# Layer 0 of a two-layer decoder from the output projection to the experts as one pipeline over token tiles, with dense experts on one-hot masked rows

## Chip, cores and metric

The kernel runs on one NeuronCore of a Trainium2 chip. The metric is the device time of one execution in microseconds (us). Engines are written as in the profile: PE (matrix multiply; PEld is its weight load), DVE (vector), ACT (activation), POOL (GpSimd), SP (the queue that issues most DMAs).

## What is computed

The input x is 2 x 1024 tokens of 256 features in fp32. Two decoder layers follow each other; each is self-attention, cross-attention on 77 context tokens, and a mixture of 8 experts. Layer 0, cut to what the change touches:

```python
x = x + L0_attn(_layernorm(x))          # ... @ Wo + bo at its end
# cross-attention: 16 heads of 16, 77 keys, only the 32 largest scores of each row count
scores = einsum('bhsd,bhnd->bhsn', Q, K) / SCALE
topk_scores, idx = top_k(scores, 32)
x = x + (softmax(topk_scores) @ V[idx]) @ Wo.T + bo
# experts: the router picks one of 8 for each token
h = _layernorm(x)
probs = softmax(h @ router_w.T + router_b)
y = (h @ expert_w[argmax(probs)].T + expert_b[argmax(probs)]) * max(probs)
x = x + y
```

Layer 1 (causal attention, cross-attention with a layer norm, experts with a hidden layer of 1024) is not changed, apart from the first step of its first layer norm.

## The kernel before, in words

The 2048 tokens are T = 16 tiles of 128. All tensors of the chip's memory are pieces of one big tile `arena`; all matmul results go to `banks`, 8 banks of 128 x 512 fp32. Every engine has its own list of instructions, in the order in which the code emits them, and waits by named counters (`sem(...)`); there is no scheduler. Layer 0 after the attention consists of five stages, and in most of them every tile is finished before the next stage begins:

1. `project(block, 0)`: per tile PE turns the attended rows (L1087), ACT copies them (L1108), PE multiplies with Wo (L1098), DVE adds the result to x (L1115) and takes the row statistics (L402).
2. `ln(block, "ln1", ...)`: for all 16 tiles mean and variance (L418), root on ACT (L438), normalized rows h (L425), turned on PE (L470) and copied to hT (L441); `add_bias` adds the output bias to x on POOL (L486).
3. `cross(block, 0, top=True)`: a pipeline over tiles. PE makes queries (L1183) and scores (L1193), ACT copies the scores to `sc` (L1291). DVE finds the 32 largest of each head in `largest`: four rounds of `max` (L1359: the 8 largest of 77) and `match_replace` (L1364: strike them out), 16 heads each. Its result is `left`, the scores without the 32. POOL subtracts the maximum from both (L1316), ACT takes exp of both (L1298, L1279), and POOL subtracts one from the other (L1326), which leaves the weights of the 32. PE turns these in four groups of four heads (L1203), ACT copies each group (L1271), PE multiplies with V (L1212), turns the result (L1221), DVE divides by the sum (`normalize`, L1388 and L1395), and PE, ACT do the output projection (L1231 to L1239, L1308, L1310). DVE, ACT and POOL run tiles 4 to 13 in a hardware loop (`Fori`) of two tiles a round; PE's list is written out.
4. `ln(block, "ln2", ..., router=0)`: as ln1, with statistics of its own pass (L415), and router logits (L450, L457).
5. `moe(block, 0, ...)`: router choice and the position of every token in an order sorted by expert (DVE, L1612 to L1676), a scatter of the rows to DRAM (`sorted`, POOL L1684), then 23 tiles of sorted rows: load, turn (L1774), multiply with the expert's weights (L1812), bias (L1813), store to `expert_out`; and a gather back (POOL L1697), with gate and addition to x on DVE (L1867) and row statistics for ln3 (L402).

Then all engines meet at a barrier, and layer 1 begins with `ln(block, "ln3", ...)`.

Of the kernel before, what the change touches and what calls it, by code (L numbers as in the profile page):

```python
# [17 lines left out]
ALU = mybir.AluOpType  # L18
# [3 lines left out]
P = 128  # L22
# [5 lines left out]
C = 77  # L28
# [64 lines left out]
def build(nc, a, out):  # L93
    ctx = ExitStack()
    with ctx:
# [19 lines left out]
        xs_dram = [scratch(f"sorted{l}", [NS * P, D]) for l in range(2)]  # L115
        ys_dram = [scratch(f"expert_out{l}", [NS * P, D]) for l in range(2)]
# [18 lines left out]
        hmask = R.f32(8)  # L135
        wr = [R.f32(KD * E).rearrange("p (k e) -> p k e", k=KD) for _ in range(2)]
# [35 lines left out]
        CONST = 16  # L172
        W1_IN = 16 * 2
        ZW = 1024
        XS_CLEAR = 16 * 2 * -(-NS * D // ZW)


        def prepare(block):
# [6 lines left out]
            def _(sp):  # L185
# [28 lines left out]
                for l in range(2):  # L214
                    rows = xs_dram[l].rearrange("(p r) d -> p (r d)", p=P)
                    for n0 in range(0, NS * D, ZW):
                        w = min(ZW, NS * D - n0)
                        sp.dma_start(rows[:, n0:n0 + w], zero_tile[:, 0:w]).then_inc(sem("xs_clear"), 16)
# [3 lines left out]
            def _(pool):  # L222
# [3 lines left out]
                pool.memset(hmask, 1.0).then_inc(sem("const"), 1)  # L226
                for l in range(2):
                    pool.memset(xv[l][:, :, :, 0:HD], 0.0).then_inc(sem("const"), 1)
                    pool.memset(xv[l][:, :, :, HD:SLOT], 1.0).then_inc(sem("const"), 1)
# [4 lines left out]
                pool.wait_ge(sem("const"), 9)  # L234
# [11 lines left out]
                pool.wait_ge(sem("const"), 14)  # L246
# [873 lines left out]

        def cross(block, l, top):
# [369 lines left out]
        def moe(block, l, free_sem, free_val):  # L1491
# [187 lines left out]
            def _(pool):  # L1679
# [3 lines left out]
                for t in range(T):  # L1683
                    pool.indirect_dma_start(  # L1684
                        out=xs_dram[l], out_offset=bass.IndirectOffsetOnAxis(ap=posi[:, t:t + 1], axis=0),
# [8 lines left out]
                for t in range(T):  # L1694
                    if t >= NY:
                        pool.wait_ge(sem(s + "_x"), t - NY + 1)
                    pool.indirect_dma_start(  # L1697
                        out=yg[t % NY], out_offset=None, in_=ys_dram[l],
# [31 lines left out]
            def _(sp):  # L1730
                sp.wait_ge(sem(s + "_sc"), 16 * T)

                def load(t, r):
                    if late(t - NTB + 1):
                        sp.wait_ge(sem(s + "_tp"), t - NTB + 1)
                    sp.dma_start(xs[r], tile_rows(xs_dram[l], t)).then_inc(sem(f"{s}_xs{r}"), 16)

                def store(t, r):
                    if big:
                        sp.wait_ge(sem(s + "_yb"), t + 1)  # L1740
                        sp.dma_start(tile_rows(ys_dram[l], t), yb[r]).then_inc(sem(f"{s}_yst{r}"), 16)
# [85 lines left out]
            def _(act):  # L1827
                def step(t, r):
# [16 lines left out]
                    if not big and inside(t):  # L1845

                        act.wait_ge(sem(s + "_yb"), t + 1)
                        act.dma_start(tile_rows(ys_dram[l], t), yb[r]).then_inc(sem(f"{s}_yst{r}"), 16)
# [26 lines left out]
        with nc.Block() as block:  # L1875
# [54 lines left out]
```

## Time and profile before

| | us |
|---|---|
| median of 3 runs (lowest, highest) | 2024.06 (2022.25, 2025.41) |
| the profiled execution | 2022.71 |
| its span in the trace | 2020.9 |
| DVE busy over the span | 1287.8 (64%) |
| PE busy over the span | 1428.5 (71%) |
| ACT busy, POOL busy | 844.4, 412.3 |
| mean granted clock of PE | 0.855 of full speed |

The span runs from the first to the last instruction of the profiled execution; 1.8 us lie around it. Matmuls are pipelined, so the busy time of PE is not its work alone. The granted clock of PE has two levels, 1.00 (2.4 GHz) and 0.50 (1.2 GHz); a value between them is a mean over time.

### The profile page before, as it was taken

To read this page: it belongs to the slowest core of one execution; us is meant where nothing else is said; L and a number is where in the kernel's file an instruction comes from. 1 tells how busy PE (TensorE), PEld (TensorE's weight loads), DVE (VectorE), ACT (ScalarE), POOL (GpSimd) and SP (SyncE) were. 2 spreads that over 40 slices of the span, in tenths; PEclk is the share of its full clock that TensorE was granted. 3 is DMA by queue.
4 is the path that set the end of the run, shared out by engine and by line. 5 is a ranking of instruction groups with operands and counts; after the bars stand their busy time and mean duration, and the time that the engine had idled before them with its cause. 6 is when DMAs were issued, how large, how long until landed. Compare 5 with 4: busy or idle time off the path is not lost. (4 is left out here: it accounts for less than half of the span.)

```text
span 2020.9 us, 26349 instructions
## 1 busy us (share of the span) xinstructions
PE 1428.5 (71%) x8174; PEld 732.7 (36%) x8175; DVE 1287.8 (64%) x4686; ACT 844.4 (42%) x1674; POOL 412.3 (20%) x338
## 2 busy tenths in 40 slices
PE   4758999999884444444355395899987883379993
PEld 2421222222243333333233252333336672146662
DVE  6988878877328999999942446677744557501112
ACT  2731777777753232222221160566674562112110
POOL 2760000000003222222203333111111333200003
PEclk9965999999996776777776695899998996689997
DMA  7175133330000000000013349245400021650103
GB/s 252 58 200 76 23 47 45 46 45 9 24 1 1 1 1 1 1 1 1 1 43 112 91 140 172 38 68 69 59 2 0 12 40 35 240 169 27 31 23 91
DMA packets 122600, 116.09 MB, mean 57 GB/s; under 512 B 47010, under 2 KB 95966, under 8 KB 122468
## 3 DMA queue, kind: packets, MB, share of 16 engines
q1 hardware_dynamic: 116087, 103.12, 23.2%
q0 software_dynamic: 3072, 8.39, 1.4%
q10 hardware_dynamic: 3312, 3.02, 0.4%
q8 instruction: 62, 1.02, 0.2%
q14 instruction: 67, 0.55, 0.1%
HBM read 72.74 MB, written 41.49 MB: 57 GB/s over the span
## 5 line engine op out<-in xcount | busy, mean ns | idle before, releaser
L1051 DVE TENSOR_REDUCE arena<-banks 128x2 f32<-128x1024 f32 (+1 forms) x448 | 481.3, 1108 | 148.4 <-PE banks L898 93.3
L987 ACT ACTIVATE arena<-banks 128x512 f32<-128x512 f32 (+3 forms) x896 | 439.2, 556 | 186.5 <-PE banks L937 180.0
L898 PE MATMUL banks<-arena 96*128 96x512 bf16 (+3 forms) x896 | 285.7, 396 | 50.2 <-DMA arena<-v 22.2
L937 PE MATMUL banks<-arena 98*128 98x512 bf16 (+3 forms) x896 | 270.8, 362 | 9.9 <-ACT arena L987 7.5
L1203 PE MATMUL banks<-arena 128*77 128x128 f32 x512 | 85.8, 323 | 213.2 <-POOL arena L1326 207.0
L949 PE MATMUL banks<-arena 128*32 128x512 f32 (+3 forms) x1792 | 219.9, 563 | 12.8 <-ACT arena L987 6.7
L1364 DVE MATCH_REPLACE8 arena<-arena 128x77 f32<-128x77 f32 x1024 | 213.7, 223 | 0.0
L1316 POOL TENSOR_TENSOR arena<-arena 128x1232 f32<-128x1232 f32 x48 | 108.7, 2264 | 370.0 <-DVE arena L1364 258.3
L898 PEld LDWEIGHTS banks<-arena 96*128 96x128 bf16 x896 | 80.2, 102 | 233.8 <-DVE arena L1051 135.5
L1858 DVE COPY arena<-banks 128x1024 f32<-128x1024 f32 x23 | 28.2, 1225 | 205.0 <-PE banks L1797 205.0
L1359 DVE MAX8 arena<-arena 128x8 f32<-128x77 f32 x1024 | 149.5, 224 | 9.4 <-issue 7.3
L1203 PEld LDWEIGHTS banks<-arena 128*77 128x77 f32 x512 | 74.1, 180 | 224.5 <-POOL arena L1326 210.5
L937 PEld LDWEIGHTS banks<-arena 98*128 98x128 bf16 x896 | 81.9, 98 | 188.2 <-ACT arena L987 124.3
L486 POOL TENSOR_TENSOR arena<-arena 128x4096 f32<-128x4096 f32 x3 | 26.9, 8980 | 492.9 <-DVE arena L425 473.7
L1812 PE MATMUL banks<-arena 128*128 x460 | 111.8, 390 | 2.2 <-DVE arena L1858 1.4
L1271 ACT COPY arena<-banks 77x512 f32<-77x512 f32 x128 | 70.2, 584 | 100.1 <-PE banks L1203 100.1
L470 PE MATMUL banks<-arena 128*128 128x128 f32 x192 | 39.2, 372 | 100.6 <-DVE arena L425 99.7
L1193 PE MATMUL banks<-arena 128*128 128x308 f32 (+2 forms) x256 | 93.5, 519 | 4.6 <-ACT arena L1264 2.4
L1812 PEld LDWEIGHTS banks<-arena 128*128 128x128 f32 x460 | 84.7, 192 | 23.0 <-issue 12.7
L1015 POOL TENSOR_SCALAR_AFFINE_SELECT arena<-arena 128x512 f32<-128x512 f32 x64 | 40.6, 635 | 248.2 <-ACT arena L987 248.2
L1697 POOL DMA_INDIRECT arena<-expert_out,arena x32 | 31.4, 983 | 275.3 <-DMA expert_out<-arena 266.2
L1785 PE MATMUL banks<-arena 128*128 x184 | 84.7, 604 | 0.3 <-issue 0.3
(213 smaller groups left out, 2007.8 us busy)
## 6 DMA issues: line engine op xcount, KB each, us to landing
arena<-parts SPq DMA_DIRECT2D x192, 128.0 KB, 7.2
arena<-in_L_ffn_W SPq DMA_DIRECT2D x16, 1024.0 KB, 12.0
parts<-arena SPq DMA_DIRECT2D x24, 512.0 KB, 8.4
v<-arena SPq DMA_DIRECT2D x32, 256.0 KB, 2.3
arena<-v SPq DMA_DIRECT2D x16, 512.0 KB, 10.9
arena<-sorted SPq DMA_DIRECT2D x46, 128.0 KB, 2.1
sorted<-arena SPq DMA_DIRECT2D x10, 512.0 KB, 8.2
expert_out<-arena ACTq DMA_DIRECT2D x23, 128.0 KB, 2.3
```

The lines of the kernel that those rows point to most:

```text
L898: mm = pe.matmul(bank[:, 0:w], qst[r][0:KS, j, i * P:(i + 1) * P], kst[r][0:KS, j, kb * BANK:kb * BANK + w], start=True, stop=not diag)
L937: pe.matmul(bank, kst[r][0:KM, j, kt * P:(kt + 1) * P], qst[r][0:KM, j, half * BANK + lo:(half + 1) * BANK], start=True, stop=True).then_i ...
L949: mm = pe.matmul(PS[SLOT * j:SLOT * (j + 1), 7, lo:BANK], vst[u % NST][:, kt, j, :], prob[:, gi % 2 * G + j, lo:BANK], start=(kt == 0), st ...
L987: act.activation(prob[:, gi % 2 * G + j, lo:BANK], PS[:, 4 + n % 3, 0:BANK - lo], ACT.Exp, scale=SCALE).then_inc(sem(s + "_exp"), 1)
L1051: dve.tensor_reduce(m2[u % 2][:, 2 * pair:2 * pair + 2, i, kb], PS[:, 2 * (n % 2):2 * (n % 2) + 2, 0:w], AX.X, ALU.max).then_inc(sem(s + " ...
L1193: mm = pe.matmul(PS[:, bank, col:col + hn * C], qt[r][:, h0 // 8, :], kb.rearrange("p j c -> p (j c)"), start=True, stop=True)
L1203: mm = pe.transpose(PS[0:C, WB + c % 2, j * P:(j + 1) * P], ex[r][:, c * 4 + j, :], ident)
L1316: return pool.tensor_tensor(dst, src, m8[r][:, 0, :, 0:1].to_broadcast([P, NH, C]), ALU.subtract)
L1359: dve.max(m8[r][:, k, hd, :], src).then_inc(sem(s + "_m" if k == 0 else f"{s}_m{k}"), 1)
L1364: dve.match_replace(out=left[r][:, hd, :], in_to_replace=m8[r][:, k, hd, :], in_values=src, imm_value=LOWEST).then_inc(sem(f"{s}_k{k}" if ...
L1785: pe.matmul(PS[:, 2 + half, :], xsT[r][:, k, :], W1[:, bass.ds(e * (KD * F) + k * F + half * BANK, BANK)], start=(k == 0), stop=False)
L1812: pe.matmul(ps, lhs[:, k, :], W[:, bass.ds(e * (nk * D) + k * D, D)], start=(k == 0), stop=False)
```

## The change

`project`, `ln1`, `add_bias`, `cross`, `ln2` and `moe` of layer 0 are taken out and a new function `cross_experts` stands in their place, one pipeline over steps t = -3 to 19. In step t, the output projection works on tile t+3, the first layer norm on t+2, queries and scores on t+1, `largest` on t, the softmax and the weights on t-1, the output projection of the cross-attention on t-2, the second layer norm on t-3, and router and experts on t-4. All lists are written out, without a hardware loop.

The experts are computed without sorting: POOL multiplies the normalized rows of a tile with the one-hot choice, which gives 8 blocks of 256 columns that are zero where the token has another expert (`hm`, 128 x 2048), PE turns the 16 pieces (`turn_spread`), ACT copies them to `hmT`, and PE multiplies all 16 with the 8 experts' weights into one sum (`experts`); the bias comes from a matmul of the turned one-hot rows. The weights (2 MB) are loaded when the attention has ended, turned on PE and kept in place of `hT`. The rows of x for ln1 and ln2 are normalized on POOL, the root is taken on ACT for one tile at a time.

One buffer `sorted` and one `expert_out` are left (layer 1 uses them), so only one is cleared at the start. `ln3` takes its row statistics in a pass of its own, after the barrier.

```diff
-            project(block, 0)
-            ln(block, "ln1", "p0_x", T, stats_due=False)
-            add_bias(block, "ln1", xb_out, "w_in", W_IN)
-            cross(block, 0, top=True)
-            ln(block, "ln2", "x0_xd", T, router=0)
-            moe(block, 0, "x0_xd", T)
+            cross_experts(block)
 ...
-            ln(block, "ln3", "e0_x", T, stats_due=False)
+            ln(block, "ln3", "e0_x", T)
+        def cross_experts(block):
+                sp.wait_ge(sem(at + "_red"), NU * (len(fills(False)) + 3))
+                for e in range(E):
+                    sp.dma_start(raw[:, e], a["L0_ffn_expert_w"][e]...).then_inc(sem(s + "_we"), 16)
+            # PE
+                def turn_expert(e):
+                    if e == 0:
+                        pe.wait_ge(sem(s + "_we"), 16 * (E + 1))
+                def turn_h2(t):
+                    pe.wait_ge(sem(s + "_h2"), t + 1)
+                    pe.wait_ge(sem(s + "_hT1"), min(t + 6, T))
+                def logits(t):
+                    pe.wait_ge(sem(s + "_h2T"), t + 1)
+                def experts(t, part):
+                    if part == 0:
+                        pe.wait_ge(sem(s + "_n"), min(t + 3, T))
+                        pe.matmul(PS[:, OB, 0:D], ohT, bias, start=True, stop=False)
+                    pe.wait_ge(sem(s + "_hmT"), t * 4 + 2 * part + 2)
+                    for n in range(E * part, E * part + E):
+                        mm = pe.matmul(PS[:, OB, 0:D], hmT[:, n, :], WeT[:, n // KD, n % KD, :], ...)
+            # ACT, the end of its step
+                        copy_weights(t - 1, 2)
+                        copy_weights(t - 1, 3)
+                        exp_all(t)
+                        turned_h1(t + 2)
+                        turned_h2(t - 3)
+                        context(t - 1)
+            # POOL, its step
+                        less_max(left[(t - 1) % 2], left[(t - 1) % 2], t - 1).then_inc(sem(s + "_d2"), 1)
+                        pool.wait_ge(sem(s + "_oh"), t - 3)
+                        pool.tensor_tensor(hm, h2[n].unsqueeze(1).to_broadcast([P, E, D]),
+                                           oh[n].unsqueeze(2).to_broadcast([P, E, D]), ALU.mult)
+                        pool.tensor_tensor(ex[n], ex[n], left[n], ALU.subtract).then_inc(sem(s + "_w"), 1)
+                        normal(h1[t % 2], t, 0).then_inc(sem(s + "_h1"), 1)
+                        pool.tensor_tensor(x[:, t + 2, :], x[:, t + 2, :], xb_out, ALU.add)
+                        normal(h2[(t - 3) % 2], t, 1).then_inc(sem(s + "_h2"), 1)
+                        less_max(ex[t % 2], sc[t % 2], t).then_inc(sem(s + "_d"), 1)
+                        pool.tensor_tensor(x[:, t - 4, :], x[:, t - 4, :], yt[(t - 4) % 2], ALU.add)
+            # DVE
+                def router(t):
+                    dve.wait_ge(sem(s + "_lp"), t + 1)
+                    dve.tensor_tensor(lg[n], PS[:, QB, D:D + E], br[0], ALU.add)
+                def choose(t):
+                    dve.tensor_scalar(ta[n], lg[n], m1[n], None, ALU.subtract)
+                for t in range(FIRST, LAST):
+                        router(t - 4)
+                        row_statistics(t)
+                        choose(t - 4)
+                        aggregate(t)
+                        chosen(t - 4)
+                        largest(t, 0)
+                        sums(t - 2)
+                        inverse(t)
+                        normalize(t - 2)
+                        gates(t - 4)
+                        for k in range(1, 4):
+                            largest(t, k)
```

The list of PE in one step of the cross-attention before: a tile's queries (L1183), half of the weights' turns (L1203), scores (L1193), the other half, V (L1212), the turn of the result (L1221) and the output projection (L1231 to L1239).

```order
L1183 MATMUL banks<-arena 128x128 x4
L1203 MATMUL banks<-arena 77x128 x8
L1193 MATMUL banks<-arena 128x462
L1193 MATMUL banks<-arena 128x154
L1193 MATMUL banks<-arena 128x308 x2
L1203 MATMUL banks<-arena 77x128 x8
L1212 MATMUL banks<-arena 32x128 x16
L1221 MATMUL banks<-arena 128x128 x4
L1231 MATMUL banks<-arena 128x128 x2
L1235 MATMUL banks<-arena 128x256 x2
L1239 MATMUL banks<-arena 128x256
```

The same place in the changed kernel, the second half of a step t = 5 to 13: the turns of the masked rows (L1332), the turn of the mixed rows of tile t-2 (L1292) with its output projection (L1299, L1301), bias and expert matmuls of tile t-4 (L1340, L1343), the weights of tile t-1 (L1262), the turns of both layer norms (L1224, L1308), V (L1272) and the logits of tile t-3 (L1314).

```order
L1332 MATMUL banks<-arena 128x128 x8
L1292 MATMUL banks<-arena 128x128 x2
L1332 MATMUL banks<-arena 128x128 x8
L1299 MATMUL banks<-arena 128x256 x2
L1301 MATMUL banks<-arena 128x256
L1340 MATMUL banks<-arena 128x256
L1343 MATMUL banks<-arena 128x256 x8
L1262 MATMUL banks<-arena 77x128 x8
L1343 MATMUL banks<-arena 128x256 x8
L1262 MATMUL banks<-arena 77x128 x8
L1308 MATMUL banks<-arena 128x128 x2
L1314 MATMUL banks<-arena 128x8 x2
```

Thirty-three matmuls and turns of the experts now stand between the scores and the logits, and the logits, on which DVE's next step begins, are the last thing PE does in a step (the rows L1224 and L1272 beside the last two are left out).

DVE before, from the end of one tile to the first round of the next: the two rows of `normalize`, then `largest`.

```order
L1388 RECIPROCAL arena<-banks 128x16
L1395 TENSOR_TENSOR arena<-banks,arena 128x256
L1349 MEMSET arena 128x1
L1352 MEMSET arena 128x1
L1359 MAX arena<-arena 128x8 x16
```

DVE in the changed kernel, from the start of a step to its first round: the router (L1596, L1598, L1603 to L1607, L1612) and the statistics of two tiles (L1625, L1630).

```order
L1596 TENSOR_TENSOR arena<-banks,arena 128x8
L1598 TENSOR_REDUCE arena<-arena 128x1
L1625 BN_STATS arena<-arena 128x6 x2
L1603 TENSOR_SCALAR arena<-arena 128x8
L1604 SCALAR_TENSOR_TENSOR arena<-arena 128x8
L1607 TENSOR_REDUCE arena<-arena 128x1
L1630 BN_AGGR arena<-arena 128x2 x2
L1612 TENSOR_SCALAR arena<-arena 128x8
L1641 MEMSET arena 128x1
L1644 MEMSET arena 128x1
L1650 MAX arena<-arena 128x8 x16
```

Ten short instructions stand ahead of the first round now, and `normalize` has moved behind that round.

## Rows read from the trace of the kernel before

**Rows 1.** Stretches: us, busy us per engine, PEclk, DMA share, GB/s

```profile
618.70:1010.70 392.00, 157.28 (x1112) 118.56 (x1112) 374.96 (x3241) 114.77 (x193) 112.95 (x47) 0.72 0.00 1
1010.70:1157.20 146.50, 71.92 (x339) 44.57 (x339) 49.09 (x161) 28.17 (x63) 36.03 (x35) 0.72 0.28 85
```

The five busy times stand in the order PE, PEld, DVE, ACT, POOL, each with its count of instructions.

**Rows 2.** Waits of DVE from 618 to 1011: us, times, longest

```profile
DVE arena L1349 <- issue: 10.7, 4, 2.8
```

**Rows 3.** Timeline of DVE: start us, us, what (first round; two tiles' starts)

```profile
618.70 0.23 DVE L1359 MAX8 arena<-arena 128x8 f32<-128x77 f32 x1 [7.29 <-issue]
...
939.73 0.06 DVE L1349 MEMSET arena<- 128x1 f32 x1
...
963.67 0.06 DVE L1349 MEMSET arena<- 128x1 f32 x1
```

**Rows 4.** Groups by line over the whole span: busy us, mean ns, idle before

```profile
L1316 POOL TENSOR_TENSOR arena<-arena 128x1232 f32<-128x1232 f32 x48 | 108.7, 2264 | 370.0 <-DVE arena L1364 258.3 <-DVE arena L1376 110.9 <-DVE arena L1359 0.8
L1326 POOL TENSOR_TENSOR arena<-arena 128x1232 f32<-128x1232 f32 x16 | 44.5, 2784 | 21.4 <-ACT arena L1279 21.4
L1298 ACT ACTIVATE arena<-arena 128x1232 f32<-128x1232 f32 x32 | 39.7, 1240 | 6.4 <-POOL arena L1316 6.4
L1271 ACT COPY arena<-banks 77x512 f32<-77x512 f32 x128 | 70.2, 584 | 100.1 <-PE banks L1203 100.1
```

**Rows 5.** Timeline, DVE and POOL in layer 0's first projection

```profile
56.21 0.19 DVE L675 TENSOR_SCALAR arena<-arena 128x48 f32<-128x48 f32 x1
...
63.45 1.16 POOL L511 TENSOR_TENSOR arena<-arena 128x512 f32<-128x512 f32 x1
...
63.64 1.01 DVE L675 TENSOR_SCALAR arena<-arena 128x48 f32<-128x48 f32 x1
```

**Rows 6.** Stretches of 5 us, columns as in Rows 1 (PEclk third from right)

```profile
85.00:90.00 5.00, 3.45 (x12) 1.86 (x12) 4.93 (x7) 3.77 (x9) 3.78 (x5) 1.00 0.16 52
605.00:610.00 5.00, 3.29 (x19) 2.71 (x20) 4.65 (x20) 2.77 (x9) 0.00 (x0) 0.83 0.00 0
785.00:790.00 5.00, 0.00 (x0) 0.00 (x0) 4.87 (x39) 0.61 (x1) 2.26 (x1) 0.50 0.01 2
```

**Rows 7.** Timeline: matmuls and turns of PE, a table load of ACT

```profile
583.61 0.63 PE L912 MATMUL banks<-arena 128*128 128x128 f32 x4 [0.80 <-ACT arena L978]
...
601.29 1.89 PE L1098 MATMUL banks<-arena 128*128 128x256 f32 x8
...
606.71 5.81 PE L470 MATMUL banks<-arena 128*128 128x128 f32 x32 [3.52 <-DVE arena L425]
...
615.03 2.34 PE L1193 MATMUL banks<-arena 128*128 128x462 f32 x8 [0.71 <-ACT arena L1264]
...
622.88 1.28 ACT L1298 ACT_TABLE_LOAD   x1
...
624.18 1.23 ACT L1298 ACTIVATE arena<-arena 128x1232 f32<-128x1232 f32 x1
...
1590.81 1.04 PE L1203 MATMUL banks<-arena 128*77 128x128 f32 x8
```

**Rows 8.** Timeline: statistics, weights' DMA issues, short DVE work, around the barrier

```profile
1031.99 5.32 DVE L415 BATCH_NORM_STATS2 arena<-arena 128x6 f32<-128x256 f32 x16 [5.13 <-ACT arena L1310]
1032.35 4.02 SPq L1548 DMA_DIRECT2D arena<-in_L_ffn_expert_w  x8
...
1063.88 0.17 DVE L1662 TENSOR_TENSOR arena<-arena 128x8 f32<-128x8 f32 x1
1064.08 0.17 DVE L1663 TENSOR_SCALAR arena<-arena 128x8 f32<-128x8 f32 x1
...
1153.76 0.74 DVE L402 BATCH_NORM_STATS2 arena<-arena 128x6 f32<-128x256 f32 x2
...
1157.24 1.17 DVE L418 BATCH_NORM_AGGREGATE arena<-arena 128x2 f32<-128x6 f32 x16 [2.73 <-PEq L1893]
```

**Rows 9.** DMA's busy tenths in fortieths of 1030 to 1045 us

```profile
DMA  0000000010699999977889999997100000000000
```

More of the change, by code:

```diff
@@ L114, in build @@
         v_dram = [scratch(f"v{l}", [NU, P, TB, G * SLOT]) for l in range(2)]
-        xs_dram = [scratch(f"sorted{l}", [NS * P, D]) for l in range(2)]
-        ys_dram = [scratch(f"expert_out{l}", [NS * P, D]) for l in range(2)]
+        xs_dram = scratch("sorted", [NS * P, D])
+        ys_dram = scratch("expert_out", [NS * P, D])
         x = R.f32(T * D).rearrange("p (t d) -> p t d", t=T)
@@ L135, in build @@
         hmask = R.f32(8)
+        eps1 = R.f32(1)
         wr = [R.f32(KD * E).rearrange("p (k e) -> p k e", k=KD) for _ in range(2)]
@@ L171, in build @@
         W0_IN, XW_IN, W_IN = 16 * 12, 16 * (9 + 2 * 5), 16 * 14
-        CONST = 16
+        CONST = 17
         W1_IN = 16 * 2
         ZW = 1024
-        XS_CLEAR = 16 * 2 * -(-NS * D // ZW)
+        XS_CLEAR = 16 * -(-NS * D // ZW)
         def prepare(block):
@@ L213, in _ @@
                 sp.wait_ge(sem("zeroed"), 1)
[L214 to L218, printed above, removed]
+                rows = xs_dram.rearrange("(p r) d -> p (r d)", p=P)
+                for n0 in range(0, NS * D, ZW):
+                    w = min(ZW, NS * D - n0)
+                    sp.dma_start(rows[:, n0:n0 + w], zero_tile[:, 0:w]).then_inc(sem("xs_clear"), 16)
             @block.gpsimd
@@ L226, in _ @@
                 pool.memset(hmask, 1.0).then_inc(sem("const"), 1)
+                pool.memset(eps1, LN_EPS).then_inc(sem("const"), 1)
                 for l in range(2):
@@ L233, in _ @@
                           allow_small_or_imprecise_dtypes=True).then_inc(sem("const"), 1)
-                pool.wait_ge(sem("const"), 9)
+                pool.wait_ge(sem("const"), 10)
                 pool.affine_select(out=ident, in_=tmp, compare_op=ALU.not_equal, fill=1.0, base=0,
@@ L1684, in _ @@
                     pool.indirect_dma_start(
-                        out=xs_dram[l], out_offset=bass.IndirectOffsetOnAxis(ap=posi[:, t:t + 1], axis=0),
+                        out=xs_dram, out_offset=bass.IndirectOffsetOnAxis(ap=posi[:, t:t + 1], axis=0),
                         in_=h[:, t, :], in_offset=None).then_inc(sem(s + "_sc"), 16)
@@ L1697, in _ @@
                     pool.indirect_dma_start(
-                        out=yg[t % NY], out_offset=None, in_=ys_dram[l],
+                        out=yg[t % NY], out_offset=None, in_=ys_dram,
                         in_offset=bass.IndirectOffsetOnAxis(ap=posi[:, t:t + 1], axis=0)).then_inc(sem(f"{s}_yg{t % NY}"), 16)
```

467 lines of the change are left out of this document (463 added, 4 removed).

## Prediction

> **What bounds the kernel now.** I first asked for the stretches of layer 0 behind the attention. The attention's last turn on PE begins at 583.6 [rows 7] and the first round of `largest` at 618.7 [rows 3]: a head of 35.1 us. The loop over 16 tiles takes 392.0 us, with DVE busy 375.0 of them and PE 157.3; from there to the barrier there are 146.5 us in which no engine is busy for half the time [rows 1]. So there are three pieces with three limits: the head is a chain of stages, the loop is DVE's, and the tail is a chain of stages and DMAs. DVE's waits show what the loop loses beyond its work: 10.7 us in four waits of up to 2.8 at its MEMSET L1349, put down to issue, which are the jumps of the hardware loop [rows 2]. Two tiles' starts are 23.9 us apart [rows 3], and 16 x 23.9 = 382 plus these waits is the 392.
>
> The change shortens head and tail, and puts their work into the loop. The question is what one step of the loop then costs.
>
> **Head.** The new PE list turns the first expert's weights in its first step, so all of the pipeline waits for their DMAs. Before, these went out from 1032.35 and the busy tenths end at about 1040.8, 8.5 us later [rows 8, 9]. After the attention (issue about 585) that is 593.5. From there, tile 0 passes the projection (4 weight turns and its rest, about 3 us), the first norm (table load 1.28 [rows 7], root, reciprocal, POOL, turn, copy: about 4.5), queries and scores (2 with copy, then 2.34 [rows 7]) and the scores' copy, about 1.25 (1232 columns, for which exp took 1.24, [rows 4]). That puts the first round at 607.9, against 618.7: **-10.8**, bounds -12 and -8. Were the weights not waited for, 8 us more would go.
>
> **DVE's step.** From 23.9 it grows by the router (two short instructions, 0.4 at a pitch of 0.20), two row statistics (0.75 with the add left out, [rows 8]: 0.33 each) and a dozen short ones. One of these is not short. `choose` begins with a tensor_scalar between SBUF operands, 0.4 us into a step, while POOL has just begun `less_max`, 2.26 long [rows 4]. A tensor_scalar of DVE that takes 0.19 alone took 1.01 while POOL ran its L511, and ended when that ended [rows 5]. I take this blocking for L1603 too: the one-hot row `oh` is ready at 3.25 instead of 2.1, so +1.15. With inverse and gates (0.6) and aggregates the step is 23.9 + 0.4 + 0.75 + 0.4 + 1.15 + 0.6 + 0.6 = **27.8**; without the blocking 26.7. The loop jumps are gone. Steps 0 to 3 have no router: 23.8, 23.8, 24.7, 25.0, together 97.
>
> **PE's chain in a step.** At full clock, counted from DVE's step start S, in order of PE's list:
> - `oh` 3.25, then POOL's `hm` of 128x2048. The nearest rows are L1316, 2264 ns for 1232 elements (1.84 each), and L1326 with 2784 (2.26) [rows 4]: bounds 3.77 and 4.63. I take 3.8, since L1326 stands beside other traffic and `hm` reads broadcasts as L1316 does. Done at 7.1.
> - First half of the spread turns to 8.0. `turn_mixed` waits for DVE's `normalize`, which now stands behind the first round: 10.0. Then turns, the other half (11.2) and `output` (12.5).
> - Bias matmul and 16 rows: 8 rows of 256 columns took 1.89, of which the first 0.38, so a pitch of 0.216 [rows 7]: 3.9, to 16.4. Weights 0 and 1 (8 turns 1.04, so 4 more are 0.42, [rows 7]) to 17.25, experts' second half 20.7 with its copies' waits, weights 2 and 3 to 21.8.
> - PE now waits about 3.5 us: ACT copies the last group (0.58, [rows 4]), loads the exp table (1.28, [rows 7]), does `exp_all` (1.24, [rows 4]) and only then copies `turned_h1`, for which `turn_h2` waits: 25.35. Context 1.08, logits to 27.2.
> - DVE's router waits for the logits. At full clock the chain (27.25) is 0.6 shorter than DVE's step (27.8), and would be hidden.
>
> But the clock: after a gap of 3.52 us that ended at 606.71 [rows 7] the stretch 605 to 610 shows a granted clock of 0.83, that is a piece at 0.50; with PE busy 3.45 of 5 it was 1.00, in idle stretches 0.50 [rows 6]. The new gap of 3.5 us lies in every step right before context and logits, whose 1.85 us could take twice as long. So a step lies between 27.8 and 29.2, and I take 28.4. PE is busy 21 to 23 us of it, ACT about 15.5, POOL about 14.5 (3.8 `hm`, 2.26 twice, 2.78, and five pieces of 256 columns at 0.5).
>
> Twelve steps of 28.4 and 97 are 438, against 392: **+46**.
>
> **Tail.** Behind the last round the steps 16 to 19 have nothing to hide behind: logits to choice 1.8, `hm` 3.8, spread 2.1, experts 7.4 with the clock's loss, then second norm, copies and logits 1.3. I add these up to ends at 24.5, 44.9, 62.5 and 81.3, and 2.7 for the barrier (2.73 before, [rows 8]): 84 against 146.5, **-62.5**; bounds 76 and 92. What falls away there is the sort, the DRAM round trips and 23 tiles of experts.
>
> **The rest.** ln3 takes its statistics after the barrier: 16 bn_stats were 5.32 [rows 8], **+5.3**. One clear of `sorted` less, 3 MB in 6 DMAs at the start: 0, it lies beside the first layer norm's DVE work; were it not hidden before, 1 to 3 us less. The turns of the other weights lie in steps -2 to 0, in which PE has time.
>
> **Sum.** Span 2020.9 - 10.8 + 46 - 62.5 + 5.3 = 1998.9. Around the span lie 1.8 us: 2000.7 for the profiled execution. That was 2022.71, 1.35 under the median of 2024.06, so **2002**.
>
> **A rule weighed.** The switch to exp's table was 1.28 us long at 622.88, and the exp after it began at 624.18, 0.02 later [rows 7]. The Trainium skill ("ScalarE: Activation LUTs", section "What ACT_TABLE_LOAD costs") gives a load of 1283 ns, which the trace agrees with, and about 1.38 us of drain behind it, which this row does not show. The new list switches twice a step (root, exp). By the row the chain ends at 27.25. As a mechanism of this kernel, a switch that cost 1.38 more would end it at 28.6, with the clock's loss at about 29.4, and 12 steps at +1 make 2012 to 2014. By the page that would be each switch's price.
>
> **The rivals.**
> 1. *Neither blocking nor clock loss.* L1603 isn't held (its operand is 8 columns, that of the row [rows 5] 48), steps are 26.7, the tail 8 shorter: 2002 - 20.4 - 8 = 1974. For it: one row only shows the blocking, and in another layer's place.
> 2. *PE's chain passes DVE.* If pieces at half clock also fall into the first half (PE waits there for `hm` and `normalize`), the chain grows by 2 to 3 more: steps 30.75, 12 x 2.35 = +28, so 2030. It decides from P = 30.15 on, where the sum is 2023. [...] Against it: PE is busy 79% of the step, more than in the stretch that had 1.00.
> 3. *The other side: PE at half clock throughout.* Were the granted clock 0.50 in all of a step, as at 785 to 790 [rows 6], PE's 17 us of matmuls on the chain would be about 30, and steps 40.5: 12 x 12.1 = +145, 2147. It holds from a mean clock under about 0.85, where the chain alone reaches 30.15; the loop before had 0.72 [rows 1], but at 40% busy.
> 4. *Switches cost a drain*, above: 2012.
> 5. *Serial steps longer:* the four last steps at 25 us instead of some 20 (clock at 0.50, each link waited for): 84 becomes 106, 2024. For it: clock 0.72 in the stretch before [rows 1].
>
> **Numbers.** 0.2%, 4 us, is about what a measurement of this kernel can tell from no change: faster is below 2020, slower above 2028. The forecast (28.4, tail 84) gets 0.42, its own range 1988 to 2018. Rival 1 gets 0.15; rival 2 gets 0.24, of which 0.05 falls faster, 0.08 same and 0.11 slower, as its step goes from 29.6 to 32; rival 3 gets 0.07, rival 4 0.05, rival 5 0.07 (0.03 same, 0.04 slower). Faster is 0.42 + 0.15 + 0.05 + 0.05 = 0.67, same 0.11 and slower 0.22. The 80% range leaves out rival 3, and ends of 1 and 2: 1972 to 2050.
>
> **What would show it.** The first round stands 24 us behind the attention's last turn; with 16, the weights were not waited for. The starts of first rounds (L1641) lie 27.8 to 29.2 apart in steps 5 to 15; L1603 lasts about 1.2 instead of 0.2 while POOL's L1546 runs, and else rival 1 holds. DVE's idle time at L1596, put down to PE's L1314, is under 1.5 us a step; more is rival 2, 3 or 4, which the granted clock and the gap between table load and exp tell apart. Steps 16 to 19 last about 84 with the barrier. L1563 lasts 3.8. What makes the forecast wrong first is the length of a step: 1 us there is 12 us in the time, as much as all else.

## The result, and the profile after

The changed kernel takes 1986.01 us (median of 4 runs, 1984.09 to 1987.29); the kernel before, 2024.74 over its 4 runs. The ratio is 0.981 (95% interval 0.980 to 0.983): 38.7 us faster, where 22 were forecast (2024.06 to 2002). Of the variants below each has four executions too; one of b_pool_waits took 8141.61 us, four times the others, and is left out of its median and its ratio. The profiled execution has a span of 1985.3 against 2020.9, 35.6 less.

Stretches of the changed kernel, columns as in [rows 1]: the head (from PE's last work of the attention, about), steps 0 to 3, steps 4 to 15, the last four steps with the barrier, layer 1.

```profile
584.00:608.10 24.10, 16.41 (x66) 12.61 (x66) 2.10 (x9) 8.85 (x20) 3.66 (x4) 0.72 0.27 88
608.10:704.02 95.92, 47.97 (x287) 34.47 (x286) 94.76 (x820) 41.09 (x71) 32.56 (x19) 0.75 0.00 1
704.02:1030.26 326.24, 275.22 (x1668) 225.38 (x1668) 308.42 (x2589) 168.94 (x311) 170.57 (x92) 0.86 0.01 1
1030.26:1118.50 88.24, 64.10 (x298) 51.88 (x298) 8.05 (x45) 28.12 (x53) 25.60 (x14) 0.79 0.00 1
1118.50:1985.00 866.50, 679.31 (x4157) 381.79 (x4157) 413.32 (x745) 343.79 (x721) 165.16 (x166) 0.89 0.31 71
```

The ledger, forecast in brackets: the first round starts at 608.1 instead of 618.7, -10.6 (-10.8). The loop takes 95.9 + 326.2 = 422.2 instead of 392.0, +30.2 (+46). The tail takes 88.2 instead of 146.5, -58.3 (-62.5). The statistics pass of ln3 takes 5.24, from 1118.54 to its aggregate at 1123.78 (+5.3). What is left, -2.1, lies in layer 1 behind that and has no counterpart in the edit. The sum is -35.6.

So the forecast missed mainly in one place, the length of a step. Twelve steps of 27.2 us on average are there, where I had taken 28.4. DVE's queue, with POOL's `less_max` (L1546) ahead of one L1603, shows what sets them:

```profile
731.27 0.17 DVE L1596 TENSOR_TENSOR arena<-banks,arena 128x8 f32<-128x8 f32 x1 [0.21 <-PE banks L1314]
732.21 1.21 DVE L1603 TENSOR_SCALAR arena<-arena 128x8 f32<-128x8 f32 x1
...
758.11 2.26 POOL L1546 TENSOR_TENSOR arena<-arena 128x1232 f32<-128x1232 f32 x1 [4.86 <-DVE arena L1654]
...
758.53 0.17 DVE L1596 TENSOR_TENSOR arena<-banks,arena 128x8 f32<-128x8 f32 x1 [0.50 <-PE banks L1314]
759.47 0.93 DVE L1603 TENSOR_SCALAR arena<-arena 128x8 f32<-128x8 f32 x1
...
786.57 0.17 DVE L1596 TENSOR_TENSOR arena<-banks,arena 128x8 f32<-128x8 f32 x1 [1.59 <-PE banks L1314]
787.51 0.22 DVE L1603 TENSOR_SCALAR arena<-arena 128x8 f32<-128x8 f32 x1
```

L1546 runs from 758.11 to 760.37; L1603, which begins at 759.47 and handles 8 columns, ends with it. The more DVE waits for the logits (0.21, 0.50, 1.59), the shorter L1603 is (1.21, 0.93, 0.22). From 786.57 to 950.03, the wait is about 1.5 and the hold is gone, and the steps are 27.24 apart. The last three of the twelve are 27.87 (the clock, see below), 25.32 and 28.07 (PE's list is shorter in these two; in the last, PE waits 3.3 for the masked rows). Wait and hold are in place of each other, which makes the profile's wait look like a gain to be had. Whether it is one, the experiments tell.

PE and ACT at the end of a step, ahead of DVE's 758.53:

```profile
752.73 0.38 PE L1224 MATMUL banks<-arena 128*128 128x128 f32 x2
756.46 0.41 PE L1308 MATMUL banks<-arena 128*128 128x128 f32 x2 [3.35 <-issue]
756.80 1.08 PE L1272 MATMUL banks<-arena 77*32 77x128 f32 x32
757.81 0.68 PE L1314 MATMUL banks<-arena 128*128 128x8 f32 x4
758.84 2.05 PE L1233 MATMUL banks<-arena 128*128 128x128 f32 x8 [0.35 <-DVE arena L1596]
```

```profile
752.49 1.07 ACT L1464 COPY arena<-banks 77x512 f32<-77x512 f32 x2
753.57 1.28 ACT L1476 ACT_TABLE_LOAD   x1
754.87 1.23 ACT L1476 ACTIVATE arena<-arena 128x1232 f32<-128x1232 f32 x1
756.00 0.36 ACT L1482 COPY arena<-banks 128x256 f32<-128x256 f32 x1
```

The gap of PE is 3.35 (forecast 3.5), and made as forecast: copies, table load, exp, copy. The half-clock stretch behind it is there too, but in most steps later than I put it. Ten of the twelve steps have the gap. In eight of them the clock fell 1.4 to 1.8 us behind its end: context still at full clock (1.08), the logits (L1314) between 0.68 and 1.00 long instead of 0.61, then 0.50 over queries and scores of the next step. A steady step's end is this one:

```profile
838.69 0.41 PE L1308 MATMUL banks<-arena 128*128 128x128 f32 x2 [3.35 <-issue]
839.03 1.08 PE L1272 MATMUL banks<-arena 77*32 77x128 f32 x32
840.04 0.97 PE L1314 MATMUL banks<-arena 128*128 128x8 f32 x4
```

In two steps it fell about 1 us before the gap's end (at 782.1 and 973.3), and then context took 1.94 instead of 1.08. The first of these steps, from 758.53 to 786.57, is 28.04 long, 0.8 more than its neighbours and near my 28.4; the other is the one of 27.87. Stretches of 5 us, and the PE rows of the first place:

```profile
785.00:790.00 5.00, 4.65 (x30) 4.20 (x23) 3.36 (x25) 1.62 (x4) 3.86 (x2) 0.50 0.02 3
790.00:795.00 5.00, 5.00 (x20) 3.59 (x20) 4.91 (x45) 4.17 (x8) 5.00 (x3) 0.77 0.00 0
```

```profile
783.05 0.66 PE L1308 MATMUL banks<-arena 128*128 128x128 f32 x2 [3.35 <-issue]
783.64 1.94 PE L1272 MATMUL banks<-arena 77*32 77x128 f32 x32
785.50 1.02 PE L1314 MATMUL banks<-arena 128*128 128x8 f32 x4
```

In the head, PE waits for the experts' weights, and its next work is slow:

```profile
592.98 1.97 PE L1194 MATMUL banks<-arena 128*128 128x128 f32 x8 [5.59 <-DMA arena<-in_L_ffn_expert_b]
594.74 0.64 PE L1206 MATMUL banks<-arena 128*128 128x128 f32 x2
595.90 2.08 PE L1212 MATMUL banks<-arena 128*128 128x256 f32 x4 [0.53 <-ACT arena L1413]
```

Four rows that are 1.03 long at full clock take 2.08. They took 2.07 at 584.46 already, ahead of that wait. In the last step of the tail nothing hides PE's wait for the masked rows, and turns and experts behind it are slow (16 turns 3.76; 32 matmuls 9.20, where the loop has 7.34 for its two halves of 3.72 and 3.62):

```profile
1097.14 3.61 POOL L1563 TENSOR_TENSOR arena<-arena 128x2048 f32<-128x2048 f32 x1 [1.55 <-DVE arena L1612]
...
1100.81 3.76 PE L1332 MATMUL banks<-arena 128*128 128x128 f32 x16 [3.42 <-POOL arena L1563]
...
1105.65 9.20 PE L1343 MATMUL banks<-arena 128*128 128x256 f32 x32
```

One caution for all that follows. PE's last group of turns of the attention (L912, now L913) began at 583.61 before, and between 577.38 and 582.28 in the changed kernel and its ten variants, though no variant edits anything ahead of it. Medians therefore can carry a few us, up to 4.9 between two of these kernels, that have nothing to do with an edit; the steady steps inside the pipeline repeat to 0.02 us. Where a term is a few us, I read it between two rows of one trace.

### The profile page after: what moved, and what is told of

Same layout as the page of the kernel before. It is cut to its first block and busy times, and to the rows that moved or that the text cites. A ratio compares the mean times of both kernels' runs of the same rounds, so it can differ in the third digit from the quotient of the medians.

```text
span 1985.3 us, 27618 instructions
## 1 busy us (share of the span) xinstructions
PE 1579.4 (80%) x8891; PEld 871.2 (44%) x8892; DVE 1255.1 (63%) x4695; ACT 934.1 (47%) x1831; POOL 482.1 (24%) x386
## 3 DMA queue, kind: packets, MB, share of 16 engines
q8 instruction: 69, 1.13, 0.2%
## 5 line engine op out<-in xcount | busy, mean ns | idle before, releaser
L1549 POOL TENSOR_SCALAR arena<-arena 128x256 f32<-128x256 f32 x32 | 39.1, 1223 | 476.2 <-DVE arena L1635 476.1
L1343 PE MATMUL banks<-arena 128*128 128x256 f32 x512 | 121.0, 392 | 0.0
L1343 PEld LDWEIGHTS banks<-arena 128*128 128x128 f32 x512 | 97.9, 196 | 18.8 <-issue 4.6
L1546 POOL TENSOR_TENSOR arena<-arena 128x1232 f32<-128x1232 f32 x32 | 72.4, 2264 | 105.2 <-DVE arena L1654 105.2
L2387 PE MATMUL banks<-arena 128*128 x368 | 85.8, 385 | 1.4 <-DVE arena L2433 1.4
L1654 DVE MATCH_VALUE_LOAD arena<-arena 128x8 f32 x1024 | 85.1, 83 | 2.7
L2360 PE MATMUL banks<-arena 128*128 x184 | 85.9, 609 | 0.5 <-ACT arena L2409 0.5
L471 PE MATMUL banks<-arena 128*128 128x128 f32 x128 | 26.4, 370 | 66.9 <-DVE arena L426 66.0
L2387 PEld LDWEIGHTS banks<-arena 128*128 128x128 f32 x368 | 67.7, 189 | 19.9 <-issue 11.0
L950 PEld LDWEIGHTS banks<-arena 128*32 128x32 f32 x1792 | 35.4, 108 | 85.0 <-ACT arena L988 60.6
L2272 POOL DMA_INDIRECT arena<-expert_out,arena x16 | 16.0, 1001 | 227.3 <-DMA expert_out<-arena 222.8
```

Of the source, the lines that this page charges most:

```text
L471: mm = pe.transpose(PS[:, banks[t % NBT], k * P:(k + 1) * P], h[:, t, k * P:(k + 1) * P], ident)
L950: mm = pe.matmul(PS[SLOT * j:SLOT * (j + 1), 7, lo:BANK], vst[u % NST][:, kt, j, :], prob[:, gi % 2 * G + j, lo:BANK], start=(kt == 0), st ...
L1343: mm = pe.matmul(PS[:, OB, 0:D], hmT[:, n, :], WeT[:, n // KD, n % KD, :], start=False, stop=(n == 2 * E - 1))
L1546: return pool.tensor_tensor(dst, src, m8[t % 2][:, 0, :, 0:1].to_broadcast([P, NH, C]), ALU.subtract)
L1654: dve.match_replace(out=left[r][:, hd, :], in_to_replace=m8[r][:, k, hd, :], in_values=src[:, hd, :], imm_value=LOWEST).then_inc(sem(f"{s} ...
L2360: pe.matmul(PS[:, 2 + half, :], xsT[r][:, k, :], W1[:, bass.ds(e * (KD * F) + k * F + half * BANK, BANK)], start=(k == 0), stop=False)
```

## The experiments

All variants are of the changed kernel. **Theory 1**: a step is a ring through DVE, POOL, PE and ACT; PE's list closes it at 27.24; DVE's own work is about 25.8, plus up to 1.3 of hold at L1603 (1.5 long instead of 0.2), which shows when DVE doesn't wait. **Theory 2**: the hold is harmless and the wait at the router is the loss. Rivals of single terms stand with the runs.

### Exp early, the hold removed, and both

a_exp_early, on ACT:

```diff
                     if inside(t - 2):
                         mixed_rows(t - 2)
+                    if inside(t):
+                        exp_all(t)
                     if inside(t - 1):
                         copy_weights(t - 1, 0)
...
-                    if inside(t):
-                        exp_all(t)
                     if inside(t + 2):
                         turned_h1(t + 2)
```

> Only ACT's order changes: exp_all with its table load stands before the first copy of the weights, where ACT was idle 4.3 us, and no longer between the last of these copies and the copy of the turned rows. Theory 1 (PE's list closes the step at 27.24 us, DVE's own work is 25.76, and DVE's tensor_scalar L1603 is held while POOL's less_max runs, which the wait for the logits hides in steps 7 to 14): PE's 3.35 us gap and the half-clock stretch behind it go, DVE no longer waits at the router, but L1603 then lasts about 1.5 in every step, so a step is 27.05 and the time 1984, 2 us below the changed kernel's 1986. Theory 2 (the hold costs nothing of its own; what DVE waited for the logits is simply saved): a step of 25.8, time 1968. Theory 3 (the gap isn't what sets PE's list): 1986 and the wait stays.

b_pool_waits, on POOL:

```diff
                         pool.wait_ge(sem(s + "_topped"), t * NH)
+                        if inside(t - 4):
+                            pool.wait_ge(sem(s + "_oh"), t - 3)
                         less_max(left[(t - 1) % 2], left[(t - 1) % 2], t - 1)
```

> Only POOL changes: its less_max on what is left waits until the choice of the step (oh) is made, so it doesn't run while DVE chooses. Theory 1: L1603 is 0.22 in every step, but PE's list still sets 27.24; hm is ready 1.5 later, at S+7.7, before PE comes to it at S+8: time 1986, within 3 us. Theory 2 as well. Rival (the hold sets the steps): about 13 us less, 1973.

ab_both has both edits.

> Both edits, exp_all early on ACT and POOL's less_max after the choice. Theory 1: neither PE's gap nor the hold is left, a step is DVE's own 25.8, time 1986 - 12 x 1.45 = 1968, although each edit alone brings 0 to 2. Theory 2 (the hold is harmless): no better than the early exp alone. Rival (PE's list or hm's later end sets the step at once): 1978 to 1986.

| kernel | median, us | ratio to before (95%) | steady step, us | wait at router | L1603 |
|---|---|---|---|---|---|
| changed | 1986.01 | 0.981 (0.980, 0.983) | 27.24 | 1.5 | 0.22 |
| a_exp_early | 1977.99 | 0.977 (0.975, 0.979) | 26.96 | 0 | 1.52 |
| b_pool_waits (3 executions) | 1989.74 | 0.983 (0.981, 0.985) | 27.26 | 1.5 | 0.22 |
| ab_both | 1962.74 | 0.969 (0.968, 0.971) | 25.66 | 0 | 0.22 |

DVE's queue, two steps of a_exp_early, and POOL's `less_max` of the first of them:

```profile
782.75 0.16 DVE L1596 TENSOR_TENSOR arena<-banks,arena 128x8 f32<-128x8 f32 x1
783.68 1.52 DVE L1603 TENSOR_SCALAR arena<-arena 128x8 f32<-128x8 f32 x1
...
809.71 0.16 DVE L1596 TENSOR_TENSOR arena<-banks,arena 128x8 f32<-128x8 f32 x1
810.64 1.53 DVE L1603 TENSOR_SCALAR arena<-arena 128x8 f32<-128x8 f32 x1
```

```profile
782.91 2.26 POOL L1546 TENSOR_TENSOR arena<-arena 128x1232 f32<-128x1232 f32 x1 [5.23 <-DVE arena L1654]
```

782.91 + 2.26 = 785.17, and 783.68 + 1.52 = 785.20: L1603 ends when POOL does. The 1.5 us of waiting are gone and 1.3 of hold stand there instead. In ab_both (its router is L1598, its tensor_scalar L1605) neither is left:

```profile
801.77 0.16 DVE L1598 TENSOR_TENSOR arena<-banks,arena 128x8 f32<-128x8 f32 x1
802.70 0.22 DVE L1605 TENSOR_SCALAR arena<-arena 128x8 f32<-128x8 f32 x1
...
827.43 0.16 DVE L1598 TENSOR_TENSOR arena<-banks,arena 128x8 f32<-128x8 f32 x1
```

Theory 1 gave steps of 27.05, 27.24 and 25.8; measured are 26.96, 27.26 and 25.66. Theory 2 gave 25.8 for the first and falls: it would have made a_exp_early as fast as both. The edits alone shorten a step by 0.3 and by nothing, together by 1.6. For b_pool_waits both theories gave the same. In ab_both the steps of 801.77 and 853.10 run at a granted clock of 1.00 and those of 827.43 and 904.40 at 0.93, and all four are 25.64 to 25.68 long; in a_exp_early, where I had expected the half clock to go, it is 0.94 to 0.88 over steps that are all 26.96. Where DVE sets the step, the half clock cost nothing.

The time of a_exp_early is 8 us down where the steps explain 3. Its tail accounts for 1.4 more (1025.35 to 1112.20, 86.85), and its attention ended 2.3 earlier; this rest is no effect of the edit that I could show.

The Trainium skill ("SBUF — State Buffer", section "Who interferes with whom") says that a VectorE instruction in a 2-port mode contends with GpSimd, that whichever issues first holds the shared port pair for the whole of its instruction while the other blocks, and that tensor_scalar is among the operations that can enter such a mode. The trace agrees: L1603 is 0.22 long without POOL's instruction, and 1.52 with one that began 0.77 earlier. No run here tells which property of L1603 brings it there.

### The weights' turns two steps later

c_weights_late, the same on PE and ACT:

```diff
-                    for e in range(2 * (t - FIRST), 2 * (t - FIRST) + 2):
-                        if e < E:
+                    for e in range(3 * (t - FIRST - 2), 3 * (t - FIRST - 2) + 3):
+                        if 0 <= e < E:
```

> PE turns the experts' weights in steps -1 to 1, three a step, instead of two a step from -3 on; nothing else. Theory (the 5.59 us in which PE waits for the weights' DMAs at 587 stand in front of the whole pipeline): the first round of largest starts at about 602 instead of 608.1, time 1980. Rival (the first norm's chain or the DMAs of the weights, now beside it, hold it up as long): 1986.

1972.08 us, ratio 0.974 (0.972 to 0.976). In its trace PE goes on with tile 0 while the weights land:

```profile
582.28 0.63 PE L913 MATMUL banks<-arena 128*128 128x128 f32 x4 [0.80 <-ACT arena L979]
...
590.76 0.44 PE L1224 MATMUL banks<-arena 128*128 128x128 f32 x2 [1.58 <-POOL arena L1549]
...
597.09 1.04 PE L1194 MATMUL banks<-arena 128*128 128x128 f32 x8
```

The first round starts at 598.28, 16.0 behind the attention's last turn, as the prediction gave for this case; in the changed kernel it was 608.10 - 582.05 = 26.05. In the seven other variants, which leave the weights where they were, it is 25.5 to 26.2; in v_all and w_all_fill, which move them too, 16.0. So the weights' place was worth 10, not the 6 I expected of this run. The profile names 5.59 of it as a wait for the DMA; the rest lies in the half clock (the projection's four rows take 1.13 here, 2.08 there) and in the turns that stood in tile 0's way, and no run takes these two apart.

### Filling PE's gap

f_fill_gap is b_pool_waits with work for PE's gap; f2_fill_only has the fill and not the wait on POOL.

```diff
                         turn_h1(t + 2)
+                    if 4 <= t < T:
+                        pe.wait_ge(sem(s + "_sc"), 2 * min(t + 2, T))
+                        for _ in range(26):
+                            pe.transpose(PS[:, 0, 0:P], ident, ident)
                     if inside(t - 3):
                         turn_h2(t - 3)
```

> ab_both without its edit on ACT: POOL's less_max waits for the choice, exp_all stays where it was, and in steps 4 to 15 PE fills its 3.35 us gap ahead of the second norm's turn with 26 turns of the identity into bank 0, whose result nobody reads. The gap stays as long; only the clock behind it can change. Theory (the half-clock stretch behind the gap costs PE's list 2.4 us, in queries and scores): the list is 24.9 us, DVE's 25.65 sets the step as in ab_both, DVE no longer waits for the logits, time 1963 to 1968. Rival (the gap itself, not the clock behind it, made the list long): steps of 27.26 as in b_pool_waits, time 1986.

1987.92 us, 0.981 (0.979 to 0.983); steps of 26.96, still with a wait of 1.2 at the router. My expectation was wrong, and the rival's price too. The granted clock did rise (780 to 785 and 790 to 810 at 1.00; 785 to 790 at 0.66, where the changed kernel had 0.50), and queries and scores are shorter. But then PE stands at another link. In the step from 838.74, all of it at a granted clock of 1.00:

```profile
839.05 1.13 PE L1233 MATMUL banks<-arena 128*128 128x128 f32 x8 [0.35 <-DVE arena L1602]
...
844.48 1.13 PE L1212 MATMUL banks<-arena 128*128 128x256 f32 x4 [1.23 <-ACT arena L1417]
...
846.53 1.10 PE L1332 MATMUL banks<-arena 128*128 128x128 f32 x8 [0.38 <-POOL arena L1569]
```

PE can begin on the masked rows, which POOL now makes behind `less_max`, 7.8 us into the step, and the rest of the ring, gap included, is 19.2. What the clock gives back is taken by waits. f2_fill_only puts POOL's order back to see whether the clock matters there:

> The changed kernel with the 26 turns in PE's gap in steps 4 to 15 and no other edit: POOL's less_max runs at the step's start, so the masked rows are ready at S+6.1 and can't hold PE up as they did in f_fill_gap. Theory (the step is a ring: DVE's router, first round and normalize until S+8.1, then PE's list with its gap until the logits; the half-clock stretch lies in the part of PE's list that would wait for normalize anyway, except 0.85 us): the ring is 26.4 long and DVE's own step with the hold, 26.96, sets it; L1603 is 1.5 in every step; time 1983. Rival (the clock's loss of 2.4 us is all on the ring, and the hold harmless): 25.7, time 1967. Rival (the clock doesn't change): 27.24 and 1986.

```profile
785.19 1.13 PE L1233 MATMUL banks<-arena 128*128 128x128 f32 x8 [0.35 <-DVE arena L1600]
...
787.04 2.35 PE L1246 MATMUL banks<-arena 128*128 128x462 f32 x8
...
791.55 1.09 PE L1332 MATMUL banks<-arena 128*128 128x128 f32 x8 [0.75 <-POOL arena L1567]
794.21 0.44 PE L1292 MATMUL banks<-arena 128*128 128x128 f32 x2 [1.57 <-DVE arena L1671]
```

Queries take 1.13 instead of 2.05; PE then waits 0.75 for POOL and 1.57 for `normalize`. From 784.88 to 946.68 there are six steps of 26.97, with L1603 at 1.37 in each and a wait of 0.06 at the router: theory 1's 26.96. (The three steps ahead of them are 27.11, 28.64 and 25.81.) The time, 1987.04 (0.982, 0.979 to 0.984; single runs 1981.6 to 1989.8), doesn't resolve the 3 us that these steps are worth. The granted clock is 1.00 from 779 to 794 and from 806 to 821. So the half clock in the loop is real, and alone it is worth 0.27 us a step: what it gives back PE mostly waits for `normalize`. The hold delays `normalize` too, and 26.96 is the step of a_exp_early, so this run shows the price of the clock only with the hold in place. Without the hold, f_fill_gap was stopped by the masked rows; what the clock would be worth there stays open.

### The tail

t_fill_tail is ab_both with 28 turns of the identity on PE ahead of the spread turns in the last four steps.

```diff
                         turn_choice(t - 4)
+                        if t >= T:
+                            for _ in range(28):
+                                pe.transpose(PS[:, 0, 0:P], ident, ident)
                         turn_spread(t - 4, 0)
```

> ab_both, and in the last four steps PE makes 28 turns of the identity into bank 0 while it waits 3.4 us for POOL's masked rows. Theory (each of these steps loses 2 to 2.5 us because the spread turns run at half clock behind that wait): the four steps, 20.7 us apart, become about 18.5, time 1963 - 9 = 1954. Rival (clock follows something else, or the turns end late and hold PE up): 1963 or more.

1957.21 us, 0.967 (0.966 to 0.969). Second of the four steps:

```profile
1033.52 3.22 PE L1366 MATMUL banks<-arena 128*128 128x128 f32 x28
1037.10 1.09 PE L1332 MATMUL banks<-arena 128*128 128x128 f32 x8 [0.36 <-POOL arena L1568]
```

In ab_both 8 such turns took 1.97 and 1.91 at a granted clock of 0.50. From the last round's end to the statistics of ln3 the tail is now 1087.85 - 1008.84 = 79.0, against 1095.72 - 1006.39 = 89.3 in ab_both: -10.3, where 9 were expected. The medians differ by 5.5; the attention ended 2.1 later in this profile, and the profiled execution is the fastest of its four, ab_both's the slowest. The first of the four steps is 2.0 shorter, the two behind it 2.6 and 2.8. Here, where nothing hides it, the clock is worth 2.6 us a step on average.

### Without the experts

k_no_experts leaves out the masked rows, the spread turns and their copies and the expert matmuls of layer 0:

```diff
-                        turn_spread(t - 4, 0)
-                        turn_spread(t - 4, 1)
...
-                        pe.matmul(PS[:, OB, 0:D], ohT, bias, start=True, stop=False)
-                    pe.wait_ge(sem(s + "_hmT"), t * 4 + 2 * part + 2)
-                    for n in range(E * part, E * part + E):
-                        mm = pe.matmul(PS[:, OB, 0:D], hmT[:, n, :], WeT[:, n // KD, n % KD, :], ...)
+                    mm = pe.matmul(PS[:, OB, 0:D], ohT, bias, start=(part == 0), stop=(part == 1))
...
-                        pool.tensor_tensor(hm, ...)
```

> The changed kernel without its dense experts: POOL's masked rows, the 16 spread turns with their copies and the 16 rows of expert matmuls of each tile are left out, bias and gate stay (layer 0's experts contribute no product). Theory: in the loop they cost almost nothing, because without them DVE's own step with the hold, 26.96, takes the place of PE's 27.24: 3 us for all of it. In the last four steps they are all on the path, about 14 of 20.7 each: 56 us. Time 1927, steps 26.96, L1603 at 1.5 in every step. Rival (PE's load in the loop is what the experts cost, as its busy share suggests): steps of 23 to 24, time 1885.

1935.71 us, 0.956 (0.954 to 0.958), where 1927 was expected. Steps are 26.96 with L1603 at 1.53, DVE's own step with the hold, so dense experts cost 0.3 us a step while there is something beside them, though they keep PE busy for some 10 us of each. The tail is 1026.75 to 1068.26, 41.5 instead of 88.2: 46.7 of the experts' cost of about 50 stand in the last four steps. I had expected 56 there; copies, norm and logits of a tile still stand in line without them.

### All four edits, and the fill

v_all adds to ab_both the late weights and the masked rows in halves:

```diff
-                        pool.tensor_tensor(hm, h2[n].unsqueeze(1).to_broadcast([P, E, D]),
-                                           oh[n].unsqueeze(2).to_broadcast([P, E, D]), ALU.mult).then_inc(sem(s + "_hm"), 1)
+                        for e in range(0, E, 4):
+                            pool.tensor_tensor(hm[:, e:e + 4], h2[n].unsqueeze(1).to_broadcast([P, 4, D]),
+                                               oh[n][:, e:e + 4].unsqueeze(2).to_broadcast([P, 4, D]), ALU.mult).then_inc(sem(s + "_hm"), 1)
...
-                    if c == 0:
-                        pe.wait_ge(sem(s + "_hm"), t + 1)
+                    if c % 2 == 0:
+                        pe.wait_ge(sem(s + "_hm"), 2 * t + c // 2 + 1)
```

> Four edits together: exp_all early, less_max after the choice, weights turned from step -1 on, and the masked rows in two halves with an increment each, so that PE turns the first four experts' rows while POOL makes the others. Theory: 1963 (both of the first) - 10 (head, as measured alone) - 1.8 x 4 = 7 for the halves in the last four steps = 1946; steps in the loop 25.65 as in ab_both. Rival (the halves are given back in a longer half-clock stretch or wait at the second half): 1953.

1950.38 us, 0.964 (0.962 to 0.965). Read in the trace, the terms are as expected: the first round 16.0 behind the attention's last turn (579.58 to 595.57), steps of 25.66, tail 1080.46 - 998.78 = 81.7, 7.6 less than ab_both's. The median is 4.4 above my number and nearer to the rival's 1953; in the profiled execution the attention ended 2.2 later than in ab_both, which no edit explains. Of the medians alone one could not say that the halves brought their 7.

w_all_fill adds 13 turns of the identity in the last four steps.

> v_all, and 13 turns of the identity into bank 0 in each of the last four steps, while PE waits 1.6 us for the first half of the masked rows. Theory (the last steps' spread turns run at half clock after that wait, and 28 such turns took 2.6 us from each in t_fill_tail): about 2 us less for each of the four, 1950.4 - 8 = 1942. Rival (the wait is already too short to cost the clock): 1950.

1941.16 us (1937.94 to 1947.37), 0.959 (0.957 to 0.962), where 1942 was expected: the fastest that does all of the work, 83 us under the kernel before and 45 under the changed one. Its stretches:

```profile
579.78:595.78 16.00, 10.91 (x54) 7.63 (x54) 2.78 (x11) 6.71 (x16) 3.67 (x4) 1.00 0.40 132
595.78:998.90 403.12, 315.68 (x1980) 251.63 (x1980) 397.51 (x3407) 210.59 (x387) 204.45 (x123) 0.88 0.01 1
998.90:1072.30 73.40, 58.99 (x342) 49.52 (x342) 7.54 (x46) 26.59 (x51) 26.18 (x18) 0.93 0.00 1
```

Head -10.0, loop 403.1 instead of 422.2, -19.0, tail 73.4 instead of 88.2, -14.8: together -43.9, and the medians differ by 44.8. DVE is busy 397.5 of the loop's 403.1; to shorten the loop much further, DVE needs less work.

## Why the prediction was right, and where not

**Sign and range**: 1986 lies in the stated range of 1972 to 2050 and 2 us under the likeliest case's own, 1988 to 2018. "Faster" was right with the reasons that I gave for head and tail. That the span was only 13.6 too high (1998.9 against 1985.3) is in part luck: the loop's term was 15.8 too high, the tail's 4.2 too low, and 2.1 went in layer 1 for no reason that the edit gives.

**Head, -10.8**: measured -10.6, of which 1.6 is an attention that ended earlier; by the attention's last turn 26.05 instead of 35.1 (24 was the sign given), -9.1, within the bounds of 8 to 12. The weights' landing was put at 593.5 and PE starts on them at 592.98. c_weights_late confirmed the other branch, 16 us; the step between the two is 10, where I had 8.

**DVE's step, 27.8**: the hold, put at +1.15, is 1.30 (1.52 - 0.22), shown by taking it away in ab_both. The short instructions were over-sized: from steps 0 and 1 (608.10 to 631.87, 23.77) to 25.66 without the hold they cost 1.9, where I had added 2.75. With the hold a step is 26.96, not 27.8.

**PE's chain, 27.2**: 27.24 was measured, but that the number was right is luck, since two errors cancel in it. POOL's masked rows took 3.61, not 3.8, and in the step from 813.81 the gap of PE ended after 24.9 us (838.69), not 25.35; then the turn, context and logits took 2.3 instead of 1.85, mostly because the clock fell within the logits. I said that this chain would be 0.6 shorter than DVE's step and so hidden; it was 0.3 longer, and the step was PE's. This was the mistaken step of the argument, and it was cheap because the hold and the wait replace each other. The signs that I gave show it: I had named a wait under 1.5 at L1596 and an L1603 of 1.2; in the steady steps the wait is 1.48 to 1.50 and L1603 0.22.

**The step, 28.4**: this term was mis-sized, by 1.2 a step, 14.6 of the 15.8 us by which the loop was off; the first four steps, 95.9 instead of 97, make the rest. "The new gap of 3.5 us lies in every step right before context and logits, whose 1.85 us could take twice as long": the gap is in ten of the twelve steps, but only in two did the clock fall before context (28.04 and 27.87 long). In the other eight it fell in the logits, which cost them 0.1 to 0.4, and then lay over queries and scores. f2_fill_only shows that this part had room as long as the hold was there: taking the half clock away brought 0.27 a step.

**Tail, -62.5**: -58.3; 88.2 where I had 84, inside 76 to 92. From the loop's end the routers stand at 24.3, 44.9 and 65.6, where I had 24.5, 44.9 and 62.5: the third of the four steps took 20.7 and not 17.6. That these steps lose 2.6 each by the clock is shown by t_fill_tail.

**ln3, +5.3**: 5.24 measured.

**The rivals**: 1 (no hold, no loss) falls by a_exp_early, whose L1603 is 1.52 in ten steps and 1.85 in the next three. 2 (PE's chain passes DVE) is what happened in kind, at 27.24 instead of its 30.75, so far below the 30.15 from which it would have decided. 3 (half clock throughout) would have made steps of 40.5; they are 27.2, at a clock of 0.86 in steps 4 to 15, which is just above the 0.85 that I had named. 4, a drain behind each table switch, is not there: the load at 753.57 lasts 1.28 and the exp begins at 754.87, which leaves 0.02 where the Trainium skill ("ScalarE: Activation LUTs", section "What ACT_TABLE_LOAD costs") has 1.38 more. The copy ahead of the load ends at 753.56, so no drain stands before it either. The rule and this trace differ, and here the trace decides. 5, serial steps of 25: the routers are 23.2, 20.6 and 20.7 apart.

## What to carry to other kernels

When steps of a pipeline form a ring (each engine waits for one before it, and the first for the last), write down the second-longest way round before pricing an edit: here removing a 1.5 us wait gave 0.3, because an instruction held by another engine stood behind it, and only both edits together gave 1.6. Work that fits beside the bounding engine is nearly free in the steady steps and full price in the last ones (experts: 0.3 us a step, then 47 us in four steps), so look at the drain of a pipeline first. A slow clock cost here only what lay on the ring: look at what PE waits for next before filling its gaps.

## What the runs showed of the hardware

A `tensor_scalar` of 8 columns on DVE, 0.22 alone, took 1.52 while POOL ran a tensor_tensor of 1232 columns, and ended within 0.03 us of it, in ten steps of a_exp_early and of k_no_experts alike; in the next three, where it began 0.44 behind POOL's instead of 0.77, it took 1.85 and ended with it too. [rows 5] had shown the same for 48 columns. The two bn_stats just ahead of it, also beside POOL's instruction, were not held: 0.74 in a_exp_early, 0.75 in ab_both without it.

The granted clock did not fall at one fixed place behind the gap of 3.35 us: in the changed kernel it fell about 1 us before the gap's end in two of ten steps, and in eight 1.4 to 1.8 us behind it, so that the matmuls right behind it were mostly still at full speed. Turns of the identity, whose result nobody reads, kept it up: in the tail, 28 of them in 3.22 us made the 8 turns behind them 1.09 instead of 1.97 long.

A POOL tensor_scalar of 256 columns with two per-row operands takes 1.22 us, twice the 0.64 of an addition of the same size; I had put both at 0.5. It was off the ring.
